# Two layer normalisations moved from VectorE to ScalarE, with scale and bias per token, in a post-norm attention and channel-mixing block

## The chip, the cores and the metric

One core of one Trainium2 chip runs the whole kernel. The metric is the time of one execution on the device in microseconds; the kernel before was timed three times, and the median of these counts.

## The reference

A batch of 16 sequences of 512 tokens with 128 channels goes through two sublayers. Each adds its input to its output and then normalises every token over its channels, without learned scale or shift:

```python
def _layernorm(x, axis=-1, eps=1e-05):
    m = jnp.mean(x, axis=axis, keepdims=True)
    v = jnp.var(x, axis=axis, keepdims=True)
    return (x - m) / jnp.sqrt(v + eps)
...
x = _layernorm(x + attn(x))      # 16 heads of 8 channels, causal softmax
x = _layernorm(x + ffn(x))       # token shift, r = sigmoid(xr Wr), relu(xk Wk)^2, r * (k Wv)
```

`attn` is multi-head attention with biases and an output projection. `ffn` mixes each token with the one before it per channel (`mu_r`, `mu_k`), and multiplies a sigmoid gate with a squared-ReLU path. Everything is float32.

## The kernel before, in words

The kernel is written by hand, one instruction stream per engine, with semaphores between them. It is a software pipeline over the 16 batch elements. Step b (from -3 to 17) handles six stages of different batch elements at once: X (load and transpose x) of element b+3, A (queries and keys) of b+2, S (scores for the row maxima) of b+1, T (transposed scores, exponentials, product with the values) of b, D (normalising the attention, projection, first layer normalisation) of b-1, and E (the feed-forward part and the second layer normalisation) of b-2. So full steps, with all of S, T, D and E, are those from 2 to 14; step 1 has D but no E, step 15 has no S, and steps 16 and 17 have D and E alone or E alone.

A step has 10 groups, 0 to 9, each with four chunks of 128 x 512 scores. The order inside a group is written out by hand in each engine's `step`:

- TensorE: two chunks of transposed scores (`tps`, L515), the mask matmuls (L538) and the scores for two row maxima (`sps`, L553), one small matmul job of the other stages; then the same for the other two chunks; at the end the product with the values (`ops`, L580) of the group before. Which small job comes where is the table `SPARE_USES`: `project` in group 5, the transposes `hT` in group 8.
- ScalarE: an exponential per chunk (`probs`, L677), two of them, then the copies due at this place, then two more. After group 9 two instructions `scaled` (L693) for the token shift.
- VectorE: a row maximum (`rowmax`, L747) per chunk of S, two, then other work, then two more. The first normalisation (y to `h`) stands after the first two row maxima of group 7, the second (z to `result`) after those of group 9. Each is four instructions on 128 x 128, one for each 128 tokens: `(src - mean) * rstd` with both as scalars per partition (L798).
- GpSimd: the causal mask of the exponentials (L850), the adds of residuals (`z`, `xbias`), the token-shift differences and sums, and `inverse_deviation`: `vareps = var + eps` (L870), then `rstd = vareps ** -0.5` (L872), for h in group 6, for z in group 7.
- SP issues the DMAs: loads of x, the bounce of queries, keys and maxima through device memory, and the store of `result`.

Both score buffers `tps` and `sps` have three banks. So two new chunks can be written when all but the last of the chunks before them have been read: chunks n and n+1 of `tps` wait until n-2 has gone through its exponential, and those of `sps` until n-2 has gone through its row maximum:

```python
wait(pe, exp_done, bank_free(n + 1))
...
wait(pe, s_reduced, bank_free(n + 1))
```

Each engine runs its own stream strictly in order, so an instruction put between two exponentials delays every later exponential by its own time, and a row maximum that is late delays the mask matmul of the next pair on TensorE with all that follows there.

Of the kernel before, what the change touches and what calls it, by code (L numbers as in the profile page):

```python
# [27 lines left out]
ACT = mybir.ActivationFunctionType  # L28
# [3 lines left out]
P = 128  # L32
# [53 lines left out]
def active(stage, b):  # L86

    return 0 <= b + OFFSET[stage] < BATCH


def before(stage, b):

    return min(max(b + OFFSET[stage], 0), BATCH)
# [77 lines left out]
def block_program(nc, x, W1, b1, Wp, bp, Wr, Wk, Wv, mu_r, mu_k, consts, out):  # L171
    with ExitStack() as ctx:
        def sb(name, shape, dt=F32):
            return ctx.enter_context(nc.sbuf_tensor(name, shape, dt))
# [4 lines left out]
        def sem(name):  # L179
            return ctx.enter_context(nc.semaphore(name))  # L180
# [41 lines left out]
        moments = sb("moments", [P, 2, TT, 2])  # L222
        vareps = sb("vareps", [P, 2, TT])
        rstd = sb("rstd", [P, 2, TT])
        h = sb("h", [P, 2, TT, E])
        hT = sb("hT", [P, SEQ + 1])
        step_d = sb("step_d", [P, SEQ])
# [53 lines left out]
        stats_done = sem("stats_done")  # L281
        moments_done = sem("moments_done")
        vareps_done = sem("vareps_done")
        rstd_done = sem("rstd_done")
        h_done = sem("h_done")
        step_done = sem("step_done")
# [11 lines left out]
        def wait(eng, semaphore, value):  # L298

            if value > 0:  # L300
                eng.wait_ge(semaphore, value)

        def is_written(eng, use, n, taken=None):

            if 0 <= n < BATCH and spare_bank(use, n) != taken:
                eng.wait_ge(spare_written[spare_bank(use, n)], COUNTS[use, n] + 1)
# [301 lines left out]
        def _(act):  # L608
# [76 lines left out]
            def split_middle(n, i):  # L685
                is_read(act, "qk"[i], n)
                nc.scalar.copy(part(i, 1), qk_rest[:, i, :]).then_inc(qk_middle, 1)  # L687

            def scale_steps(n):
                wait(act, step_done, n + 1)  # L690
                wait(act, mixed_done, 2 * n)
                for i in range(2):
                    nc.scalar.activation(scaled[:, i, :], step_d[:], ACT.Copy, scale=mus[:, i:i + 1])\  # L693
                        .then_inc(scaled_done, 1)

            def step(b):
                if b == 1 - OFFSET["A"]:
                    act.wait_ge(first_out[1], 16)
                    load_operand(act, b % 2 ^ 1, 0, 1, 1)
                    setup_rest()  # L700
                for g in range(GROUPS):
                    tb, tg = late(b, g)
                    for place in range(2):
                        if active("T", tb):
                            exp_chunk_of(before("T", tb), tg, 2 * place)
                            exp_chunk_of(before("T", tb), tg, 2 * place + 1)
                        for _, use, n in ORDER[b, g, place]:
                            spare_use(use, n)
                        if place == 0 and tg == 1 and active("D", tb):
                            copy_o(before("D", tb), 1)  # L710
                        if place == 0 and tg == CHUNKS + 1 and active("T", tb):
                            copy_o(before("T", tb), 0)
                    if g in (1, 2) and active("A", b) and before("A", b) > 0:
                        split_middle(before("A", b), g - 1)
                    if g in (0, 1) and active("A", b) and before("A", b) == 0:
                        split_middle(0, g)
                    if tg == 9 and active("D", tb):
                        scale_steps(before("D", tb))
# [5 lines left out]
        def _(dve):  # L724
# [35 lines left out]
            def spare_use(use, n):  # L760
                if use not in ("q", "k", "sums0", "sums1", "project", "value"):
                    return
                k = spare_bank(use, n)
                spare = spares[k]
                if use in ("q", "k"):
                    i = "qk".index(use)
                    wait(dve, qk_high, 2 * n + i + 1)
                    wait(dve, qk_split, 2 * (n - 1) + i + 1)
                    last = nc.vector.scalar_tensor_tensor(qk_rest[:, i, :], spare[:], bias[:, i:i + 1], part(i, 0),  # L769
                                                          ALU.add, ALU.subtract)  # L770
                elif use in ("sums0", "sums1"):

                    half = int(use[-1])
                    is_written(dve, use, n)
                    is_written(dve, "attnT", n - 1, k)
                    tiles = spare[:].rearrange("q (t r s h d) -> q s t r h d", t=TT, r=QUARTET, s=2, h=2)
                    nc.vector.reciprocal(inv[:, half], tiles[:, 1, :, :, :, 0]).then_inc(inv_done, 1)  # L777
                    wait(dve, inv_done, 2 * n + half + 1)
                    for t in range(TT):
                        last = nc.vector.tensor_tensor(  # L780
                            attn[:, t, DH * half:DH * half + DH].rearrange("q (r h) d -> q r h d", h=2),
                            tiles[:, 0, t], inv[:, half, t].unsqueeze(3).to_broadcast([P, QUARTET, 2, DH]), ALU.mult)
                elif use == "project":
                    wait(dve, xbias_done, n + 1)
                    is_written(dve, use, n)
                    last = nc.vector.tensor_tensor(y[:].rearrange("p t e -> p (t e)"), spare[:],
                                                   xbias[:].rearrange("p t e -> p (t e)"), ALU.add)
                elif use == "value":
                    wait(dve, z_done, n)
                    is_read(dve, "gate", n, k)  # L790
                    is_written(dve, use, n)
                    last = nc.vector.scalar_tensor_tensor(gated[:], gate[:], 1.0, spare[:], ALU.add, ALU.mult)  # L792
                last.then_inc(spare_read[k], 1)

            def normalise(i, n, src, dst, done_rstd, done):
                wait(dve, done_rstd, n + 1)
                for t in range(TT):
                    last = nc.vector.tensor_scalar(dst[:, t, :], src[:, t, :], moments[:, i, t, 0:1],  # L798
                                                   rstd[:, i, t:t + 1], ALU.subtract, ALU.mult)
                last.then_inc(done, 1)  # L800

            def step(b):
                for g in range(GROUPS):
                    tb, tg = late(b, g)
                    if active("S", b):
                        reduce_chunk(before("S", b), g, 0)
                        reduce_chunk(before("S", b), g, 1)
                    for _, use, n in ORDER[b, g, 0]:
                        spare_use(use, n)
                    if tg == 7 and active("D", tb):  # L810
                        n = before("D", tb)
                        wait(dve, z_done, n - 1)
                        normalise(0, n, y, h[:, n % 2], rstd_done, h_done)
                    if tg == 9 and active("E", tb):
                        n = before("E", tb)
                        wait(dve, stored, 16 * n)
                        normalise(1, n, z, result, rstd2_done, result_done)
                    if tg == 5 and active("D", tb):
                        n = before("D", tb)
                        is_read(dve, "project", n)  # L820
                        layer_norm_moments(y, 0, n, stats_done, moments_done)
                    if tg == 6 and active("E", tb):
                        n = before("E", tb)
                        wait(dve, z_done, n + 1)
                        layer_norm_moments(z, 1, n, stats2_done, moments2_done)
                    if active("S", b):
                        reduce_chunk(before("S", b), g, 2)
                        reduce_chunk(before("S", b), g, 3)
                    for _, use, n in ORDER[b, g, 1]:
                        spare_use(use, n)  # L830
# [5 lines left out]
        def _(pool):  # L836
# [22 lines left out]
            def split_max(n, half):  # L859
# [5 lines left out]
                nc.gpsimd.tensor_tensor(negmax_parts[:, 1, :], negmax[:], negmax_parts[:, 0, :], ALU.subtract)\  # L865
                    .then_inc(max_split, 1)

            def inverse_deviation(i, n, done_moments, done_eps, done_rstd):
                wait(pool, done_moments, n + 1)
                nc.gpsimd.tensor_scalar(vareps[:, i, :], moments[:, i, :, 1], EPS, None, ALU.add).then_inc(done_eps, 1)  # L870
                wait(pool, done_eps, n + 1)
                nc.gpsimd.tensor_tensor(rstd[:, i, :], vareps[:, i, :], half_power[:], ALU.pow).then_inc(done_rstd, 1)  # L872

            def mix_step(n):

# [77 lines left out]
```

## Time and profile before

| | |
|---|---|
| median of 3 runs | 742.22 us (741.91 to 744.46) |
| the profiled execution | 745.85 us, of which the span from first to last instruction is 744.1 us |
| TensorE / VectorE / ScalarE / GpSimd busy | 614.7 / 548.4 / 471.2 / 372.3 us |
| granted TensorE clock, mean | 0.963 of 2.4 GHz |
| one full step (period) | 40.17 us, from 264.64 to 304.81 |

Busy time counts instructions of an engine that overlap once. A row of the timeline gives the start in us, the length of the merged piece, the engine and line, the operation, output and inputs with shapes, a count, and in brackets how long the engine had been idle just before and what released it. A row of the chain gives start, length and what ran. PE is TensorE, DVE is VectorE, ACT is ScalarE, POOL is GpSimd.

### The profile page before, as it was taken

The page shows a single profiled execution, that of the slowest core. Times are in us where ns is not written, and L with a number is a line of the kernel's source. Part 1 is how long each engine was busy: PE and PEld are TensorE (multiplying, and loading weights), DVE is VectorE, ACT ScalarE, POOL GpSimd, SP SyncE. Part 2 cuts the span into 40 slices and gives each one's busy share as a digit, 9 for nine tenths or more (in the row PEclk, how much of TensorE's full clock was granted, in tenths as well). Part 3 has the DMA queues.
Part 4 walks back from the last instruction along what each step waited for, and adds up shares of the span by engine and source line. Part 5 has one row for each costly group of instructions (what it writes and reads, how often), then busy time and mean ns, then how long its engine had stood idle before and what let it go on. Part 6 is the DMA issues. An engine that isn't in the chain of part 4 may idle for free.

```text
span 744.1 us, 18019 instructions
## 1 busy us (share of the span) xinstructions
PE 614.7 (83%) x6727; PEld 277.9 (37%) x6727; DVE 548.4 (74%) x1642; ACT 471.2 (63%) x916; POOL 372.3 (50%) x519
## 2 busy tenths in 40 slices
PE   4468887898989899898989898989989898977643
PEld 2132333343443434353434344343434343433232
DVE  1477784879798888889797979888887979782231
ACT  2104773777768686767677776867686767677510
POOL 3011342455656565555655565646555565455623
PEclk9999997999999999999999999999999999999855
DMA  3421313131414223232313141413223231100100
GB/s 115 92 88 45 102 46 114 29 114 36 119 44 118 57 69 107 60 115 59 117 42 118 39 115 43 126 50 80 95 61 115 58 104 40 37 18 17 30 14 15
DMA packets 66014, 53.25 MB, mean 72 GB/s; under 512 B 11333, under 2 KB 61830, under 8 KB 65926
## 3 DMA queue, kind: packets, MB, share of 16 engines
q1 hardware_dynamic: 65198, 51.83, 25.2%
q8 instruction: 53, 0.87, 0.5%
q10 hardware_dynamic: 728, 0.26, 0.2%
q14 instruction: 35, 0.29, 0.1%
HBM read 34.70 MB, written 17.30 MB: 70 GB/s over the span
## 4 chain that ended last, share of the span: by engine, by line
PE 55%; DVE 18%; ACT 8%; issue 6%; POOL 6%; DMA 5%; SPq 1%; ACTq 1%; POOLq 0%; DVEq 0%
PE ops L580 14%; DVE rowmax L747 12%; PE sps L553 10%; PE tps L515 9%; PE spare L441 8%; ACT probs L677 5%; PE spare L459 4%; PE sps L538 3%; DVE h L798 3%; DMA xres<-L_attn_x 2%; POOL probs L850 2%; PE spare L491 2%; POOL mixed L883 2%; PE spare L475 2%; DMA d_max<-negmax_parts 1%
## 5 line engine op out<-in xcount | busy, mean ns | idle before, releaser
L747 DVE TENSOR_REDUCE rowmax<-sps 128x1 f32<-128x512 f32 (+7 forms) x1024 | 401.9, 450 | 101.6 <-PE sps L553 101.1
L677 ACT ACTIVATE probs<-tps 128x512 f32<-128x512 f32 x640 | 346.5, 596 | 147.1 <-PE tps L515 147.1
L850 POOL TENSOR_SCALAR_AFFINE_SELECT probs<-probs 128x512 f32<-128x512 f32 x256 | 158.8, 638 | 256.6 <-ACT probs L677 256.5
L580 PE MATMUL ops<-probs,vop 128*32 128x384 f32 (+3 forms) x2048 | 173.5, 446 | 8.1 <-POOL probs L850 6.8
L515 PE MATMUL tps<-qop,kop 50*128 50x384 bf16 (+3 forms) x1024 | 126.5, 305 | 40.3 <-ACT probs L677 36.5
L553 PE MATMUL sps<-kop,qop 48*64 48x512 bf16 (+7 forms) x2048 | 130.4, 310 | 8.4 <-DMA kop<-d_parts 8.4
L538 PE MATMUL sps<-qmask,dup 64*128 64x128 bf16 (+1 forms) x640 | 69.7, 214 | 33.0 <-DVE rowmax L747 28.7
L515 PEld LDWEIGHTS tps<-qop,kop 50*128 50x128 bf16 x1024 | 34.2, 94 | 161.3 <-ACT probs L677 115.2
L580 PEld LDWEIGHTS ops<-probs,vop 128*32 128x32 f32 x2048 | 50.7, 110 | 82.4 <-issue 61.4
L553 PEld LDWEIGHTS sps<-kop,qop 48*64 48x64 bf16 x2048 | 43.1, 106 | 50.5 <-issue 19.3
L538 PEld LDWEIGHTS sps<-qmask,dup 64*128 64x128 bf16 x640 | 31.4, 95 | 75.2 <-DVE rowmax L747 68.7
L857 POOL TENSOR_TENSOR qk_parts<-qk_rest,qk_parts 128x512 bf16<-128x512 f32 x32 | 36.9, 1153 | 29.4 <-ACT qk_parts L687 29.4
L459 PE MATMUL spare<-xT,w1p 128*128 128x512 f32 x62 | 39.6, 725 | 2.7 <-ACT xT L639 2.7
L883 POOL TENSOR_TENSOR mixed<-scaled,hT 128x512 f32<-128x512 f32 x32 | 39.9, 1272 | 0.8 <-ACT scaled L693 0.8
L769 DVE SCALAR_TENSOR_TENSOR qk_rest<-spare,bias,qk_parts 128x512 f32<-128x512 f32 x31 | 23.3, 752 | 21.4 <-ACT qk_parts L655 21.4
L655 ACT ACTIVATE qk_parts<-spare,bias 128x512 bf16<-128x512 f32 x31 | 21.3, 687 | 26.2 <-PE spare L459 26.2
L907 POOL TENSOR_TENSOR xbias<-xres,bias 128x512 f32<-128x512 f32 x16 | 20.3, 1268 | 33.9 <-DMA xres<-L_attn_x 33.9
L872 POOL TENSOR_TENSOR rstd<-vareps,half_power 128x4 f32<-128x4 f32 x32 | 33.4, 1043 | 2.7
L792 DVE SCALAR_TENSOR_TENSOR gated<-gate,spare 128x512 f32<-128x512 f32 x16 | 11.0, 688 | 31.2 <-PE spare L441 31.2
L777 DVE RECIPROCAL inv<-spare 128x32 f32<-128x32 f32 x32 | 11.2, 349 | 21.3 <-PE spare L475 21.3
L914 POOL TENSOR_TENSOR z<-gated,h 128x512 f32<-128x512 f32 x16 | 20.3, 1267 | 12.1 <-DVE gated L792 12.1
L491 PE MATMUL spare<-mixed,wffT 128*128 128x512 f32 x32 | 19.9, 705 | 6.0 <-POOL mixed L883 6.0
(72 smaller groups left out, 585.2 us busy)
## 6 DMA issues: line engine op xcount, KB each, us to landing
d_parts<-qk_parts SPq DMA_DIRECT2D x15, 768.0 KB, 3.7
qop<-d_parts SPq DMA_DIRECT2D x192, 32.0 KB
qop<-d_parts SPq DMA_DIRECT2D x64, 96.0 KB
kop<-d_parts SPq DMA_DIRECT2D x189, 32.0 KB
kop<-d_parts SPq DMA_DIRECT2D x63, 96.0 KB
xa<-L_attn_x SPq DMA_DIRECT2D x16, 256.0 KB, 3.0
xres<-L_attn_x SPq DMA_DIRECT2D x16, 256.0 KB, 3.4
out<-result SPq DMA_DIRECT2D x16, 256.0 KB, 2.5
```

Of the source, the lines that this page charges most:

```text
L441: last = nc.tensor.matmul(spare[:, P * t:P * t + P], tokensT[:, P * t:P * t + P], weights, start=True, stop=True)
L459: last = nc.tensor.matmul(spare[:], w1p[:, "qk".index(use), :], xT[:, par], start=True, stop=True)
L491: last = nc.tensor.matmul(spare[:], wffT[:, 1, :], mixed[:, 1, :], start=True, stop=True)
L515: last = nc.tensor.matmul(tps[:, bank(n + k), off:off + w], kop[r, par, pair, BLK * a:BLK * a + BLK], qop[r, par, pair, BLK * a:SEQ], star ...
L538: nc.tensor.matmul(dst, dup[r, :], src, start=True, stop=False, skip_group_check=True)
L553: last = nc.tensor.matmul(sps[out:out + QBLK, bank(n + k), off:off + w], qop[r, par, pair, QBLK * a:QBLK * a + QBLK], kop[r, par, pair, 0: ...
L580: last = nc.tensor.matmul(ops[32 * t:32 * t + 32, BLK * a:SEQ], vop[:, par, a, QUARTET * half + t, hh, :], probs[:, g % 2, i, off:off + w] ...
L677: nc.scalar.activation(probs[:, g % 2, i, :], tps[:, bank(n), :], ACT.Exp, scale=SCALE)\
L747: last = nc.vector.reduce_max(rowmax[:, par, QUARTET * half + i, a:a + 1], sps[:, bank(n), off:off + w], axis=AX_X)
L850: last = nc.gpsimd.affine_select(out=v, in_=v, compare_op=ALU.is_ge, fill=0.0, base=0, pattern=[[0, QUARTET], [1, BLK]], channel_multiplie ...
L857: nc.gpsimd.tensor_tensor(part(i, 2), qk_rest[:, i, :], part(i, 1), ALU.subtract).then_inc(qk_split, 1)
L883: nc.gpsimd.tensor_tensor(mixed[:, i, :], scaled[:, i, :], hT[:, 0:SEQ], ALU.add)\
```

## The change

The four instructions of each normalisation move from VectorE's stream to ScalarE's, in the same groups (7 and 9) and behind the first two exponentials there. They become an Identity activation `rstd * src + shift`, where `rstd` and `shift` are operands of one number per partition. GpSimd makes `shift = -(mean * rstd)` behind each `rstd`, by two more operations on 128 x 4 elements, each waiting for the one before on a new semaphore `powered`; `rstd_done` is now raised by the last of them. VectorE's add that writes y (`project`) gains a wait for the previous `h_done`, since y is now read by another engine. The waits for a free `h` or `result` buffer move to ScalarE with the instructions.

```diff
+            def normalise(i, n, src, dst, done_rstd, done):
+                wait(act, done_rstd, n + 1)
+                for t in range(TT):
+                    last = nc.scalar.activation(dst[:, t, :], src[:, t, :], ACT.Identity, bias=shift[:, i, t:t + 1],
+                                                scale=rstd[:, i, t:t + 1])
+                last.then_inc(done, 1)
...
                         for _, use, n in ORDER[b, g, place]:
                             spare_use(use, n)
+                        if place == 0 and tg == 7 and active("D", tb):
+                            n = before("D", tb)
+                            wait(act, z_done, n - 1)
+                            normalise(0, n, y, h[:, n % 2], rstd_done, h_done)
+                        if place == 0 and tg == 9 and active("E", tb):
+                            n = before("E", tb)
+                            wait(act, stored, 16 * n)
+                            normalise(1, n, z, result, rstd2_done, result_done)
...
                     is_written(dve, use, n)
+                    wait(dve, h_done, n)
                     last = nc.vector.tensor_tensor(y[:].rearrange("p t e -> p (t e)"), spare[:],
...
-            def normalise(i, n, src, dst, done_rstd, done):
-                wait(dve, done_rstd, n + 1)
-                for t in range(TT):
-                    last = nc.vector.tensor_scalar(dst[:, t, :], src[:, t, :], moments[:, i, t, 0:1],
-                                                   rstd[:, i, t:t + 1], ALU.subtract, ALU.mult)
-                last.then_inc(done, 1)
...
-                    if tg == 7 and active("D", tb):
-                        n = before("D", tb)
-                        wait(dve, z_done, n - 1)
-                        normalise(0, n, y, h[:, n % 2], rstd_done, h_done)
-                    if tg == 9 and active("E", tb):
-                        n = before("E", tb)
-                        wait(dve, stored, 16 * n)
-                        normalise(1, n, z, result, rstd2_done, result_done)
...
-                nc.gpsimd.tensor_tensor(rstd[:, i, :], vareps[:, i, :], half_power[:], ALU.pow).then_inc(done_rstd, 1)
+                nc.gpsimd.tensor_tensor(rstd[:, i, :], vareps[:, i, :], half_power[:], ALU.pow).then_inc(powered, 1)
+                wait(pool, powered, count)
+                nc.gpsimd.tensor_tensor(shift[:, i, :], moments[:, i, :, 0], rstd[:, i, :], ALU.mult).then_inc(powered, 1)
+                wait(pool, powered, count + 1)
+                nc.gpsimd.tensor_scalar(shift[:, i, :], shift[:, i, :], -1.0, None, ALU.mult).then_inc(done_rstd, 1)
```

ScalarE's order from group 6 to the start of the next step, in a full step, before (names are the kernel's tensors, output first, then the inputs; x6 is a count):

```order
L639 COPY xT<-spare 128x512
L677 ACTIVATE probs<-tps 128x512 x6
L662 COPY hT<-spare 128x512
L677 ACTIVATE probs<-tps 128x512 x6
L693 ACTIVATE scaled<-step_d,mus 128x512 x2
L677 ACTIVATE probs<-tps 128x512 x4
```

and the same place in the changed kernel:

```order
L641 COPY xT<-spare 128x512
L679 ACTIVATE probs<-tps 128x512 x2
L694 ACTIVATE h<-y,shift,rstd 128x128 x4
L679 ACTIVATE probs<-tps 128x512 x4
L664 COPY hT<-spare 128x512
L679 ACTIVATE probs<-tps 128x512 x4
L694 ACTIVATE result<-z,shift,rstd 128x128 x4
L679 ACTIVATE probs<-tps 128x512 x2
L702 ACTIVATE scaled<-step_d,mus 128x512 x2
L679 ACTIVATE probs<-tps 128x512 x4
```

The h group now stands behind two of the four exponentials of group 7, the result group behind two of the four of group 9, ahead of `scaled` and the next step's exponentials.

VectorE's order over the same groups, before:

```order
L753 BN_STATS stats<-z 128x6 x4
L757 BN_AGGR moments<-stats 128x2 x4
L747 TENSOR_REDUCE rowmax<-sps 128x1 x8
L798 TENSOR_SCALAR h<-y,moments,rstd 128x128 x4
L747 TENSOR_REDUCE rowmax<-sps 128x1 x12
L777 RECIPROCAL inv<-spare 128x32
L780 TENSOR_TENSOR attn<-spare,inv 128x64 x4
L747 TENSOR_REDUCE rowmax<-sps 128x1 x2
L798 TENSOR_SCALAR result<-z,moments,rstd 128x128 x4
L747 TENSOR_REDUCE rowmax<-sps 128x1 x6
```

and in the changed kernel:

```order
L770 BN_STATS stats<-z 128x6 x4
L774 BN_AGGR moments<-stats 128x2 x4
L764 TENSOR_REDUCE rowmax<-sps 128x1 x20
L794 RECIPROCAL inv<-spare 128x32
L797 TENSOR_TENSOR attn<-spare,inv 128x64 x4
L764 TENSOR_REDUCE rowmax<-sps 128x1 x8
```

Both groups have left VectorE, and the row maxima around them are neighbours now.

GpSimd's order in groups 6 and 7, before:

```order
L870 TENSOR_SCALAR vareps<-moments 128x4
L872 TENSOR_TENSOR rstd<-vareps,half_power 128x4
L850 AFFINE_SELECT probs<-probs 128x4x128 x2
L863 TENSOR_SCALAR negmax_parts<-negmax 32x128
L865 TENSOR_TENSOR negmax_parts<-negmax,negmax_parts 32x128
```

and in the changed kernel:

```order
L877 TENSOR_SCALAR vareps<-moments 128x4
L879 TENSOR_TENSOR rstd<-vareps,half_power 128x4
L881 TENSOR_TENSOR shift<-moments,rstd 128x4
L883 TENSOR_SCALAR shift<-shift 128x4
L853 AFFINE_SELECT probs<-probs 128x4x128 x2
```

The two operations for shift stand between rstd and the next mask of probs; the same holds for z's rstd in group 7.

## Rows read from the trace of the kernel before

**Rows 1.** The page: busy times, and the chain's shares by engine.

```profile
PE 614.7 (83%) x6727; PEld 277.9 (37%) x6727; DVE 548.4 (74%) x1642; ACT 471.2 (63%) x916; POOL 372.3 (50%) x519
...
PE 55%; DVE 18%; ACT 8%; issue 6%; POOL 6%; DMA 5%; SPq 1%; ACTq 1%; POOLq 0%; DVEq 0%
```

**Rows 2.** The chain of waits in order of time: start, us, what (VectorE, group 7).

```profile
135.83 1.45 DVE h L798 x4
...
256.43 1.35 DVE h L798 x4
257.78 0.67 DVE rowmax L747 x2
...
657.86 1.35 DVE h L798 x4
```

**Rows 3.** Timeline of TensorE, groups 8 and 0 of one period.

```profile
257.33 0.39 PE L515 MATMUL tps<-qop,kop 50*128 50x384 bf16 x4
258.50 0.23 PE L538 MATMUL sps<-qmask,dup 64*128 64x128 bf16 x2 [0.78 <-DVE rowmax L747]
...
259.59 0.39 PE L515 MATMUL tps<-qop,kop 50*128 50x384 bf16 x4
259.92 0.23 PE L538 MATMUL sps<-qmask,dup 64*128 64x128 bf16 x2
...
266.41 0.39 PE L515 MATMUL tps<-qop,kop 50*128 50x512 bf16 x2 [0.92 <-ACT probs L677]
```

**Rows 4.** Timeline of ScalarE, groups 7 and 9 of the same period.

```profile
254.48 2.16 ACT L677 ACTIVATE probs<-tps 128x512 f32<-128x512 f32 x4 [0.60 <-PE tps L515]
...
262.49 2.16 ACT L677 ACTIVATE probs<-tps 128x512 f32<-128x512 f32 x4 [1.22 <-PE tps L515]
264.54 1.33 ACT L693 ACTIVATE scaled<-step_d,mus 128x512 f32<-128x512 f32 x2
```

**Rows 5.** Groups of instructions on ScalarE: count, busy us and mean ns, idle before.

```profile
L626 ACT ACTIVATE wffT<-tps 128x128 f32<-128x128 f32 x1 | 0.3, 285 | 0.0
L693 ACT ACTIVATE scaled<-step_d,mus 128x512 f32<-128x512 f32 x32 | 21.3, 721 | 1.1 <-POOL step_d L877 1.1
L687 ACT CAST qk_parts<-qk_rest 128x512 bf16<-128x512 f32 x32 | 19.8, 618 | 2.0 <-DVE qk_rest L769 2.0
L655 ACT ACTIVATE qk_parts<-spare,bias 128x512 bf16<-128x512 f32 x31 | 21.3, 687 | 26.2 <-PE spare L459 26.2
L677 ACT ACTIVATE probs<-tps 128x512 f32<-128x512 f32 x640 | 346.5, 596 | 147.1 <-PE tps L515 147.1
```

**Rows 6.** Timeline of GpSimd, group 6 of the next period.

```profile
289.69 0.23 POOL L870 TENSOR_SCALAR vareps<-moments 128x4 f32<-128x4 f32 x1
290.00 1.05 POOL L872 TENSOR_TENSOR rstd<-vareps,half_power 128x4 f32<-128x4 f32 x1
293.65 1.23 POOL L850 TENSOR_SCALAR_AFFINE_SELECT probs<-probs 128x512 f32<-128x512 f32 x2 [2.60 <-ACT probs L677]
```

**Rows 7.** Step 15 on ScalarE and TensorE, and the last h in the chain.

```profile
689.75 2.16 ACT L677 ACTIVATE probs<-tps 128x512 f32<-128x512 f32 x4 [0.54 <-PE tps L515]
...
691.73 0.39 PE L515 MATMUL tps<-qop,kop 50*128 50x384 bf16 x4
...
720.14 1.13 DVE h L798 x4
```

**Rows 8.** Stretches: length, busy time of PE, PEld, DVE, ACT, POOL, granted clock, DMA.

```profile
264.73:266.41 1.68, 0.76 (x13) 0.31 (x10) 1.37 (x4) 1.68 (x4) 1.68 (x3) 1.00 0.51 146
...
697.95:699.45 1.50, 0.03 (x4) 0.03 (x5) 0.00 (x0) 1.33 (x3) 1.31 (x3) 1.00 0.49 151
699.45:701.25 1.80, 1.75 (x16) 0.56 (x16) 0.00 (x0) 0.00 (x0) 1.80 (x2) 0.55 0.55 162
...
119.97:129.86 9.89, 9.89 (x65) 5.29 (x66) 4.41 (x13) 2.82 (x6) 3.03 (x5) 0.51 0.26 79
284.59:290.42 5.83, 5.63 (x65) 3.23 (x64) 4.65 (x14) 2.82 (x6) 3.64 (x6) 1.00 0.53 120
```

More of the change, by code:

```diff
@@ L224, in block_program @@
         rstd = sb("rstd", [P, 2, TT])
+        shift = sb("shift", [P, 2, TT])
         h = sb("h", [P, 2, TT, E])
@@ L283, in block_program @@
         vareps_done = sem("vareps_done")
+        powered = sem("powered")
         rstd_done = sem("rstd_done")
@@ L866, in split_max @@
                     .then_inc(max_split, 1)
+            powers = [0, 0]
             def inverse_deviation(i, n, done_moments, done_eps, done_rstd):
+                count = 2 * (powers[i] + powers[1 - i]) + 1
+                powers[i] = n + 1
                 wait(pool, done_moments, n + 1)
```

## The prediction

> **What bounds the kernel now.** I read the page first [rows 1]: TensorE is busy for 83% of the span, VectorE for 74%, ScalarE for 63%, and the chain that ended last is TensorE for 55% and VectorE for 18%. No engine is saturated; the time is a ring of short waits around TensorE, repeated in a period of 40.2 us. So the question is not how much work leaves VectorE, but which waits end on it. The chain of waits in order of time [rows 2] shows one: the four instructions that normalise h lie on the chain once in each of the 14 periods from 135.8 to 657.9 us, with the row maxima queued behind them. The timeline of TensorE [rows 3] shows the cost. After the score matmuls of 257.33 the mask matmul starts at 258.50, idle for 0.78 us for VectorE; with no wait that step takes 259.92 - 259.59 = 0.33 us, so the whole stall is 258.50 - 257.33 - 0.33 = 0.84 us. The normalising of result (group 9) is never on the chain.
>
> In group 9 the ring closes over ScalarE instead. Its timeline [rows 4] shows four exponentials packed without a gap (2.16 us from 262.49), then the two scaled instructions (1.33 us), and the second pair of score matmuls of group 0 waits 0.92 us, until 266.41, for the exponential that follows them [rows 3]. What is inserted between those four exponentials reaches TensorE undiminished.
>
> **The change part by part.** All times are those of the period from 254 to 295 us.
>
> *Price of one normalising ACTIVATE.* No row has 128 columns and both pointers; I build it from rows [rows 5]. 128 columns without pointers take 285 ns. A scale per partition adds 721 - 618 = 103 ns, a bias per partition 687 - 596 = 91 ns. Both: 479 ns. Neighbours overlap: the four exponentials give (2.16 - 0.596)/3 = 0.52 us from start to start, 0.08 less than one lasts; the two scaled ones 1.33 - 0.72 = 0.61, which is 0.11 less. With 0.10 an ACTIVATE costs 0.38 us, four delay the next instruction by 1.52 us, and the last of four ends 3 x 0.38 + 0.48 = 1.62 us after the first starts. Bounds: 0.29 us (four 1.16) if the pointers are fetched together, 0.42 us (four 1.68) if reading SBUF adds 20 ns and only 0.08 overlaps. I take 0.38, because both increments are measured, each alone.
>
> The Trainium skill, page "ScalarE: Activation LUTs", section "What ACT_TABLE_LOAD costs", says that each pointer operand adds about 93 ns and that neighbours overlap by about 93 ns. By it one would cost 0.39 us, four 1.54, and the sum below would be +18.9 us in place of +18.3; no row here shows two pointers in one instruction.
>
> *Group 7, h leaves VectorE.* The row maxima after S(7) follow at once and are done by 257.1, so the mask matmul no longer waits for VectorE. But ScalarE now has h between its second and third exponential: the third started at 254.48 + 2 x 0.52 = 255.52 [rows 4]; now at 257.04, and ends 0.60 later, at 257.64. The score matmuls of group 8 need it (three banks), so they start at 257.69 and not 257.33, and the mask matmul 0.33 later at 258.02. Gain: 258.50 - 258.02 = 0.48 us of the 0.84; the new wait eats the rest. h itself ends at 255.52 + 1.62 = 257.14, before its transposes. 14 periods: **-6.7 us**.
>
> *Group 9, result goes between the exponentials.* The third exponential, the fourth, both scaled instructions and the first exponential of group 0 all stand behind it in ScalarE's queue. All move by 1.52 us and TensorE's second pair of score matmuls with them. result runs in 13 periods with both matmul streams: **+19.8 us**. What VectorE is spared there is worth nothing: no one waited for it. Net per period: +1.04 us.
>
> *Step 15* has scores but no row maxima: VectorE was not in the way, so nothing is won. The third exponential of group 7 now ends at 689.75 + 1.04 + 1.52 + 0.60 = 692.91, and the matmuls of 691.73 [rows 7] start at 692.96: +1.23; group 9 again +1.52. **+2.75 us**.
>
> *GpSimd.* Two operations on 128 x 4 elements follow each rstd. The nearest row is vareps: 0.23 us, 0.31 from its start to that of rstd [rows 6]. So +0.62 each time. For h, rstd ends at 291.05, shift at 291.67, and GpSimd then waits anyway until 293.65. For z it delays one mask of probs by 0.6 us, whose matmuls come a whole group later. Nothing in steps 1 to 15; without that cover it would be 0.62 us on the path. That happens in the tail.
>
> *Tail.* For the last batch rstd, shift, normalise stand in line twice. Each time +0.62 for shift and 1.62 - 1.12 = 0.50 for the slower four [rows 7]; result of the batch before now also delays scaled by 0.3. **+2.5 us**.
>
> *Queues and waits moved.* The store of result is SP's next item after result_done, with the operand loads behind it; result ends at most 0.2 us later than before, while the groups that use those loads move by 1.04. The project step's new wait on h_done is for the previous batch, long over; VectorE's wait for rstd is gone. Nothing for either.
>
> Sum: -6.7 + 19.8 + 2.75 + 2.5 = **+18.3 us**. The profiled execution took 745.85 us, 3.6 above the median of 742.22; the sum is added to the median: 760.5. With 0.29 us per ACTIVATE the gain is the full 0.84 (-11.8), the loss 15.1, step 15 2.0, the tail 1.5: +6.9, 749.1. With 0.42: -4.5 + 21.8 + 3.1 + 2.9 = +23.3, 765.5.
>
> *TensorE's clock.* The delay lands as a hole in TensorE's work. From the end of its PV matmuls in group 8 (264.25 in the new order) to the late score matmuls (267.45) it has 0.76 us of work, that of the row 264.73:266.41 [rows 8], and 2.4 us of idling. Near the end of the trace the clock fell from 2.4 to 1.2 GHz after a shorter hole: TensorE is busy for 0.03 us of the 1.5 after 697.95, and then the granted clock goes to 0.55 [rows 8]. The price of a fall: 65 matmuls from 119.97 took 9.89 us at clock 0.51; the same 65 take 5.83 at full clock [rows 8]: 4.06 us. So none of the 13 new holes costs a clock, or up to all do: 0 to 53 us. I take five, +20.3, between the two: the one place alike fell, and the 0.92 us wait that stands in every period before never did. **Total: 742.2 + 18.3 + 20.3 = 780.8 us.**
>
> **The rivals.**
> *The holes cost no clock.* Then 760.5 us, between 749.1 and 765.5. For it: the fall is one place in a tail where TensorE has little work anyway. Against it: the new hole is deeper than that one, and comes every period.
> The page "TensorE: Matmul & The Clock Gate" of the Trainium skill, section "Why this matters for your kernels", warns only of long idle gaps between bursts of matmuls. By that rule no new hole would cost a clock and the time is this rival's; the fall near 699.6, after 1.5 us, speaks against the rule.
>
> *Not slower: pointer fetches are hidden.* If consecutive ACTIVATEs prefetch their scale and bias, one costs 0.285 - 0.10 = 0.185 us and four 0.74. The third exponential of group 7 then never delays TensorE, and the full 0.84 us is won against 0.74 lost: -0.84 (the one period without result) - 13 x 0.10 + 1.2 (step 15) + 0.7 (tail) = -0.3 us, 742 us. The point that decides is four in 0.84 us, 0.21 each. Against it: the two scaled instructions stand 0.61 apart and exponentials of the same width 0.52, so a pointer shows even in a pair.
>
> *The change doesn't free VectorE where it counts.* If the mask matmul then waited for something else as long, the 6.7 us would be missing: 767 us without a clock. ScalarE's row makes that half true already.
>
> **How the numbers follow.** Slower with clock falls 0.55, slower without 0.33, even 0.12. The likeliest is 780.8, its own range 765 to 815 (one to thirteen falls, and a little for step 15). The whole range, 749 to 815, takes in the second case down to its cheapest ACTIVATE and leaves out the even case. A measurement tells about 0.5% (3.7 us) from no change. Slower 0.88; same 0.09; faster 0.03, from the even case with a still cheaper ACTIVATE.
>
> **What would show it.** In the lines of the new profile: h and result on ScalarE with a mean near 0.48 us, 0.38 apart. TensorE's mask matmul at the start of group 8 no longer waits for VectorE, its score matmuls wait briefly for ScalarE. The second pair of group 0 waits about 1.5 us for ScalarE, not 0.92. A period of 41.2 us where the clock stays at 1.0, about 45 where it falls; in stretches of 10 us, values near 0.5 right after group 9. ScalarE busy 471 + 128 x 0.48 = 532 us. The prediction is wrong if the period stays at 40.2, if the ACTIVATEs stand 0.2 us apart, or if a clock of 1.0 holds while the period is still far over 41.2.

## The result, and the profile after

The changed kernel is slower: a ratio of 1.0263 to the kernel before, 95% interval 1.0214 to 1.0312. The median of its six runs is 769.4 us (757.7 to 774.6), that of the kernel before, timed beside it, 745.1. The ratio leaves out runs more than 1.5% above the fastest of their kernel, here the three longest of the change. The forecast was 780.8 us, range 749 to 815, slower with 0.88.

The page of the profiled execution (763.36 us, span 761.6) answers to [rows 1]:

```profile
PE 622.0 (82%) x6727; PEld 278.0 (36%) x6727; DVE 511.2 (67%) x1514; ACT 515.8 (68%) x1044; POOL 386.1 (51%) x583
...
PE 58%; ACT 17%; DVE 11%; issue 5%; POOL 3%; DMA 3%; SPq 1%; ACTq 1%; DVEq 0%; POOLq 0%
L694 ACT ACTIVATE h<-y,shift,rstd 128x128 f32<-128x128 f32 x64 | 26.2, 487 | 9.3 <-POOL shift L883 9.3
L694 ACT ACTIVATE result<-z,shift,rstd 128x128 f32<-128x128 f32 x64 | 26.3, 488 | 7.7 <-POOL shift L883 7.7
```

VectorE has 37 us less to do and ScalarE 45 us more, and they have changed places in the chain: VectorE from 18% to 11%, ScalarE from 8% to 17%. One ACTIVATE with both pointers (`rstd` and `shift`, the operands of one number per partition) lasts 487 ns; 479 was built from [rows 5].

Where the period gained and lost shows in TensorE's timeline, groups 8 to 0, which answers to [rows 3]. The first line is the key matmul of the step's group 2, the last that of the next step; I use it as the mark of a period.

```profile
278.22 1.13 PE L493 MATMUL spare<-mixed,wffT 128*128 128x512 f32 x2
...
301.93 0.39 PE L517 MATMUL tps<-qop,kop 50*128 50x384 bf16 x4 [0.23 <-ACT probs L679]
302.15 0.22 PE L540 MATMUL sps<-qmask,dup 64*128 64x128 bf16 x2
...
305.65 0.39 PE L517 MATMUL tps<-qop,kop 50*128 50x256 bf16 x4
...
309.38 0.39 PE L517 MATMUL tps<-qop,kop 50*128 50x512 bf16 x2 [0.93 <-ACT probs L679]
...
311.48 0.39 PE L517 MATMUL tps<-qop,kop 50*128 50x512 bf16 x2 [1.34 <-ACT probs L679]
...
319.15 1.12 PE L493 MATMUL spare<-mixed,wffT 128*128 128x512 f32 x2
```

The same marks in the kernel before:

```profile
233.92 1.12 PE L491 MATMUL spare<-mixed,wffT 128*128 128x512 f32 x2
...
262.00 0.39 PE L515 MATMUL tps<-qop,kop 50*128 50x256 bf16 x4
...
274.08 1.12 PE L491 MATMUL spare<-mixed,wffT 128*128 128x512 f32 x2
```

The mask matmul of group 8 no longer waits for VectorE; the score matmuls ahead of it now wait 0.23 us for ScalarE. From the mark to the start of group 9 it was 262.00 - 233.92 = 28.08 us and is 305.65 - 278.22 = 27.43: 0.65 won. From there to the second score pair of group 0 it was 266.41 - 262.00 = 4.41 [rows 3] and is 311.48 - 305.65 = 5.83: 1.42 lost. The first pair of group 0, which did not wait before, now waits 0.93 us. These two waits, with 0.76 us of matmuls between them, are the hole behind group 9. The period grows from 40.16 to 40.93 us.

ScalarE's timeline has the cause in its order [rows 4 for before]:

```profile
298.78 1.08 ACT L679 ACTIVATE probs<-tps 128x512 f32<-128x512 f32 x2 [0.59 <-PE tps L517]
299.75 1.64 ACT L694 ACTIVATE h<-y,shift,rstd 128x128 f32<-128x128 f32 x4
301.29 2.21 ACT L679 ACTIVATE probs<-tps 128x512 f32<-128x512 f32 x4
...
306.14 1.08 ACT L679 ACTIVATE probs<-tps 128x512 f32<-128x512 f32 x2 [1.17 <-PE tps L517]
307.11 1.64 ACT L694 ACTIVATE result<-z,shift,rstd 128x128 f32<-128x128 f32 x4
308.65 1.07 ACT L679 ACTIVATE probs<-tps 128x512 f32<-128x512 f32 x2
309.61 1.33 ACT L702 ACTIVATE scaled<-step_d,mus 128x512 f32<-128x512 f32 x2
310.83 2.16 ACT L679 ACTIVATE probs<-tps 128x512 f32<-128x512 f32 x4
```

Four ACTIVATEs of 1.64 us delay the next exponential by 1.54 (299.75 to 301.29, 307.11 to 308.65), so one costs 0.385 us. Behind result stand two exponentials, scaled, and the next step's exponentials without a gap.

The third part is the clock. Of the eleven periods between steps 2 and 13, nine last 40.92 to 41.21 us and two longer, 43.70 and 42.46. These stretches of 1 us cover the hole in the second of the two (columns as in [rows 8]):

```profile
225.00:226.00 1.00, 0.07 (x6) 0.04 (x3) 0.00 (x0) 1.00 (x3) 0.00 (x0) 1.00 0.00 0
226.00:227.00 1.00, 0.75 (x8) 0.21 (x8) 0.21 (x1) 1.00 (x3) 0.60 (x2) 1.00 0.61 181
227.00:228.00 1.00, 0.00 (x0) 0.00 (x0) 1.00 (x2) 1.00 (x3) 1.00 (x3) 1.00 0.61 177
228.00:229.00 1.00, 0.91 (x8) 0.25 (x8) 0.08 (x1) 0.92 (x3) 1.00 (x2) 0.63 0.63 146
229.00:230.00 1.00, 1.00 (x5) 0.50 (x2) 0.76 (x2) 0.69 (x2) 1.00 (x1) 0.50 0.67 110
```

TensorE works 0.82 us of three, and then its clock falls from 2.4 to 1.2 GHz, for the matmuls of group 0 that are the chain. The waits are the same, to 0.01 us, as in the period shown above, in which the clock held:

```profile
225.99 0.39 PE L517 MATMUL tps<-qop,kop 50*128 50x512 bf16 x2 [0.93 <-ACT probs L679]
...
228.09 0.49 PE L517 MATMUL tps<-qop,kop 50*128 50x512 bf16 x2 [1.34 <-ACT probs L679]
```

### The profile page after: what moved, and what is told of

Read it like the earlier page. It is cut to its first block, busy times and chain, and to the rows that moved or that the text cites. A ratio compares the mean times of both kernels' runs of the same rounds, so it can differ in the third digit from the quotient of the medians.

```text
span 761.6 us, 18083 instructions
## 1 busy us (share of the span) xinstructions
PE 622.0 (82%) x6727; PEld 278.0 (36%) x6727; DVE 511.2 (67%) x1514; ACT 515.8 (68%) x1044; POOL 386.1 (51%) x583
## 4 chain that ended last, share of the span: by engine, by line
PE 58%; ACT 17%; DVE 11%; issue 5%; POOL 3%; DMA 3%; SPq 1%; ACTq 1%; DVEq 0%; POOLq 0%
PE ops L582 15%; PE spare L443 10%; PE sps L555 9%; PE tps L517 9%; ACT probs L679 8%; DVE rowmax L764 7%; PE spare L461 5%; ACT h L694 3%; PE sps L540 3%; ACT result L694 3%; PE spare L493 2%; PE spare L477 1%; ACT scaled L702 1%; PE spare L490 1%; PE spare L482 1%
## 5 line engine op out<-in xcount | busy, mean ns | idle before, releaser
L582 PE MATMUL ops<-probs,vop 128*32 128x384 f32 (+3 forms) x2048 | 176.7, 453 | 6.5 <-POOL probs L853 5.4
L517 PE MATMUL tps<-qop,kop 50*128 50x384 bf16 (+3 forms) x1024 | 128.4, 309 | 60.8 <-ACT probs L679 57.1
L540 PE MATMUL sps<-qmask,dup 64*128 64x128 bf16 (+1 forms) x640 | 70.0, 215 | 22.2 <-DVE rowmax L764 18.3
L461 PE MATMUL spare<-xT,w1p 128*128 128x512 f32 x62 | 41.5, 757 | 2.7 <-ACT xT L641 2.7
L918 POOL TENSOR_TENSOR xbias<-xres,bias 128x512 f32<-128x512 f32 x16 | 20.3, 1270 | 26.9 <-DMA xres<-L_attn_x 26.9
L694 ACT ACTIVATE h<-y,shift,rstd 128x128 f32<-128x128 f32 x64 | 26.2, 487 | 9.3 <-POOL shift L883 9.3
L694 ACT ACTIVATE result<-z,shift,rstd 128x128 f32<-128x128 f32 x64 | 26.3, 488 | 7.7 <-POOL shift L883 7.7
```

What stands on the lines that cost most here:

```text
L461: last = nc.tensor.matmul(spare[:], w1p[:, "qk".index(use), :], xT[:, par], start=True, stop=True)
L517: last = nc.tensor.matmul(tps[:, bank(n + k), off:off + w], kop[r, par, pair, BLK * a:BLK * a + BLK], qop[r, par, pair, BLK * a:SEQ], star ...
L540: nc.tensor.matmul(dst, dup[r, :], src, start=True, stop=False, skip_group_check=True)
L582: last = nc.tensor.matmul(ops[32 * t:32 * t + 32, BLK * a:SEQ], vop[:, par, a, QUARTET * half + t, hh, :], probs[:, g % 2, i, off:off + w] ...
L694: last = nc.scalar.activation(dst[:, t, :], src[:, t, :], ACT.Identity, bias=shift[:, i, t:t + 1], scale=rstd[:, i, t:t + 1])
```

## The experiments

Two theories were set against each other. A: the place of the four ACTIVATEs in ScalarE's stream decides, and the hole behind group 9 costs the clock beside it. B: the added load on ScalarE and GpSimd costs the time, wherever it stands. "Period" is the usual interval of the mark; a fall of the clock shows as a longer one.

**e1 and e2: one normalisation each.** In e1 result goes back to VectorE, in e2 h does (and with it goes the new wait on `h_done`).

```diff
-                        if place == 0 and tg == 9 and active("E", tb):   # e1: on ScalarE no longer
+                    if tg == 9 and active("E", tb):                      # e1: on VectorE
...
-                        if place == 0 and tg == 7 and active("D", tb):   # e2: likewise h
+                    if tg == 7 and active("D", tb):
```

> h is normalised on ScalarE as in the change, result on VectorE as before. Theory A (what counts is where the four ACTIVATEs stand in ScalarE's stream): the gain of the changed kernel's group 8 stays (0.65 us in each of 14 periods) and group 9's loss is gone. Period 39.5 us, no hole behind group 9 and no fall of the clock there; step 15 and the tail give 2 to 3 us back. About 6.5 us faster than before, ratio 0.991. Theory B (the load on ScalarE and the longer chain on GpSimd cost the time wherever they stand): half of the loss stays, ratio about 1.013.

> result is normalised on ScalarE between the exponentials of group 9, h on VectorE as before. Theory A: period 40.17 + 1.42 = 41.6 us, the wait of the second score pair of group 0 for ScalarE at 1.3 us, and VectorE still ahead of the mask matmul in group 8 with 0.78 us. 13 periods 18.5, step 15 and tail 3: about 21 us slower without falls of the clock, ratio 1.03; with falls up to 1.05. Theory B: half of the change's loss, ratio about 1.013.

e1: ratio 0.9912 (0.9879 to 0.9945), period 39.52 us, no fall in steps 2 to 14. e2: ratio 1.0528 (1.0468 to 1.0588); where the clock holds the period is 41.26, not 41.6, and eight of eleven are 42.8 to 44.2. Gains and losses add up: e1's 39.52 and the 1.42 of group 9 make 40.94 (the change: 40.93). For e2, the expectation left out what GpSimd's part wins by itself: the 39.85 of e6 below and 1.42 make 41.27. So the change is a good half and a bad one: h alone wins, result alone costs more than both together. B falls. One of e2's falls, around its hole and to the end of the slow stretch:

```profile
351.00:353.00 2.00, 0.76 (x8) 0.26 (x8) 1.11 (x2) 2.00 (x4) 1.49 (x3) 0.98 0.59 174
353.00:359.40 6.40, 6.20 (x40) 1.84 (x40) 2.22 (x4) 2.87 (x6) 2.78 (x3) 0.50 0.65 112
```

With these 6.4 us at half clock this period took 44.04 us, 2.8 more than 41.26; the shorter falls cost 1.5 to 1.8.

**e5, e8, e10: the hole filled.** TensorE repeats a score matmul four times in each wait of group 0, into a bank that the real one then overwrites. e5 is the change with it, e8 is e2 with it, e10 the kernel before with it.

```diff
+                if g == 0 and 2 <= batch < BATCH - 1:
+                    wait(pe, exp_done, bank_free(n))
+                    for _ in range(FILL):          # 4
+                        nc.tensor.matmul(tps[:, bank(n), :], kop[HROWS * 0:TERMS + MROWS, par, 0, 0:BLK],
+                                         qop[HROWS * 0:TERMS + MROWS, par, 0, :], start=True, stop=True)
                 wait(pe, exp_done, bank_free(n + 1))
```

> The changed kernel, and TensorE repeats a score matmul four times in each of the two waits of group 0 (steps 2 to 14), into a bank that the real matmul then overwrites. If the holes cost the clock: no fall behind group 9 in steps 2 to 14, every period 40.9 us, the median near 759 us (ratio 1.019) and the runs within some 6 us, not 17. If the clock has no part in it: median 769 and a spread as before; if the extra matmuls themselves delay, a period over 40.9.

> e2 with the repeated score matmuls of e5 in the two waits of group 0. In e2 eight of the eleven intervals between steps 2 and 13 were over 41.3 us (42.8 to 44.2). If falls of the clock made those: every interval 41.3 us, the median some 17 us lower than e2's 783, near 766. If something else made them: the same long intervals, about 783.

> The kernel before with the repeated score matmuls of e5. There is no fall of the clock behind group 9 to prevent, and the wait of 0.92 us has room for the four of them: the same time as before, ratio 0.998 to 1.004, period 40.2. If the repeats help or hurt by themselves, it differs, and e5 and e8 have to be read with that.

e5: median 761.0 us, six runs from 757.9 to 764.1 (the change: 757.7 to 774.6), periods of 40.95 us, one of 41.24, and no fall in steps 2 to 14. But its ratio, 1.0258 (1.0207 to 1.0308), can't be told from the change's 1.0263, and the two profiled executions took the same time, 763.21 and 763.36 us. The medians of all runs against those of before are 1.0246 here and 1.0326 there, so e5 points the way that was expected and does not show it. e8 does: 766.7 us where e2 took 783.2, ratio 1.0288 (1.0243 to 1.0334) against 1.0528, with ten periods of 41.24 to 41.53 and one of 42.86 instead of eight long ones. Work that computes nothing made the kernel 16 us faster. The eleven periods of e2 and of e8 as one stretch each, with the granted clock at 0.96 and at 1.00:

```profile
151.15:622.85 471.70, 417.24 (x4629) 184.04 (x4621) 360.48 (x1078) 337.14 (x672) 262.29 (x397) 0.96 0.29 77
```

```profile
155.58:611.22 455.64, 421.15 (x4716) 187.46 (x4708) 360.00 (x1078) 336.91 (x672) 261.64 (x397) 1.00 0.29 79
```

In e5, the hole looks like this:

```profile
306.78 1.03 PE L514 MATMUL tps<-qop,kop 50*128 50x512 bf16 x4
307.69 0.39 PE L523 MATMUL tps<-qop,kop 50*128 50x512 bf16 x2
...
308.38 1.03 PE L514 MATMUL tps<-qop,kop 50*128 50x512 bf16 x4
309.88 0.39 PE L523 MATMUL tps<-qop,kop 50*128 50x512 bf16 x2 [0.47 <-ACT probs L685]
```

L514 are the repeats: they fit and the wait of 1.34 is down to 0.47. e10 missed its expectation: 753.4 us, ratio 1.013 (1.0097 to 1.0163), period 40.89. I had overlooked that the kernel before has only one of the two waits; ahead of the first score pair of group 0 TensorE is busy, so four repeats of 0.2 us each lie on the path there. That is what e5 and e8 don't suffer, since their periods are those of the unfilled kernels. So filling pays only where the hole is.

**e7: no pointers.** The change with ACTIVATEs of constant scale and without bias.

```diff
-                    last = nc.scalar.activation(dst[:, t, :], src[:, t, :], ACT.Identity, bias=shift[:, i, t:t + 1],
-                                                scale=rstd[:, i, t:t + 1])
+                    last = nc.scalar.activation(dst[:, t, :], src[:, t, :], ACT.Copy, scale=1.5)
```

> The changed kernel with ACTIVATEs that have a constant scale of 1.5 and no bias, so h and result are 1.5 times y and z. If the two pointers make the price: one lasts 0.29 to 0.31 us, four delay by 0.8 and not 1.52; score matmuls of group 8 not delayed (1.0 us won), 0.7 us lost in group 9: period 39.9 us, ratio about 0.996. If it is the four instructions and their waits as such: period 40.9, ratio 1.02.

One lasts 310 ns; the pointers cost 177 ns together, close to the 194 that [rows 5] give for two fetches, so they add up and aren't shared. (The function also changes, from Identity to Copy; its share was not measured alone.) The period is 39.91 us, as expected; but seven of eleven periods are 41.4 to 41.9, with falls of the clock, and the ratio is 1.0126 (1.0069 to 1.0183), not 0.996. Here the first wait of group 0 is short and the second as long as in the change:

```profile
301.56 0.39 PE L517 MATMUL tps<-qop,kop 50*128 50x512 bf16 x2 [0.20 <-ACT probs L679]
...
303.67 0.39 PE L517 MATMUL tps<-qop,kop 50*128 50x512 bf16 x2 [1.34 <-ACT probs L679]
```

**e6 and e11: GpSimd's part alone.** Both normalisations on VectorE as before, GpSimd makes shift and no one reads it. In e11 z's two operations stand behind the mask of group 7.

```diff
                         count = inverse_deviation(1, before("E", tb), moments2_done, vareps2_done, rstd2_done)
...
                         mask_group(before("T", tb), tg)
+                    if tg == 7 and active("E", tb):       # e11
+                        make_shift(1, count, rstd2_done)
```

> Both normalisations on VectorE as before; GpSimd makes shift as in the change, and rstd_done comes only after it. If GpSimd's two operations are hidden: period 40.2 us, 1.2 us more in the tail, ratio 1.002. If they are on the path: 0.6 us in each of 14 periods, ratio 1.012.

> As e6, with z's two shift operations behind the mask of probs of group 7 on GpSimd and no longer ahead of it. The period of e6 was 39.85 us against 40.17 before, and the fourth ACTIVATE-sized piece of h on VectorE lasted about 340 ns where it lasted over 660 before. If the mask running beside it made it slow: here the mask starts as early as before, that instruction is slow again and the period is 40.17. If something else in e6 won the 0.32 us: 39.85.

e6: ratio 0.9974 (0.9941 to 1.0006), but the period is 39.85 us, 0.32 shorter than before, where 40.2 was expected. The tail pays 1.2 us, as expected. The reason for the shorter period stands in VectorE's lines. In the kernel before, and in e6:

```profile
256.35 1.43 DVE L798 TENSOR_SCALAR h<-y,moments,rstd 128x128 f32<-128x128 f32 x4
...
257.00 0.70 POOL L850 TENSOR_SCALAR_AFFINE_SELECT probs<-probs 128x512 f32<-128x512 f32 x1
```

```profile
291.78 1.11 DVE L800 TENSOR_SCALAR h<-y,moments,rstd 128x128 f32<-128x128 f32 x4
...
292.97 0.64 POOL L852 TENSOR_SCALAR_AFFINE_SELECT probs<-probs 128x512 f32<-128x512 f32 x1
```

Before, GpSimd's mask starts beside the fourth instruction of h, and the four take 1.43 us; in e6 the two new operations push the mask behind them, and the four take 1.11. e11 puts the mask back and keeps all work: period 40.24, mean of h 434 ns (e6: 363), ratio 1.002 (0.9981 to 1.0058). So it is the mask running beside h that makes it slow. One instruction of the four bears all of it, the fourth before and the third in e11; the others take about 0.34 us. Before, it ends 0.08 us behind the mask (257.78 and 257.70). The first line is from before, the second from e11:

```profile
257.11 0.67 DVE L798 TENSOR_SCALAR h<-y,moments,rstd 128x128 f32<-128x128 f32 x1
```

```profile
292.89 0.76 DVE L800 TENSOR_SCALAR h<-y,moments,rstd 128x128 f32<-128x128 f32 x1
```

One period of the kernel before shows the same without any edit: the mask started 0.93 us after h instead of 0.65, the four took 1.10 us, and the period lasted 39.84 us (475.36 to 515.20).

```profile
497.79 1.10 DVE L798 TENSOR_SCALAR h<-y,moments,rstd 128x128 f32<-128x128 f32 x4
...
498.72 0.67 POOL L850 TENSOR_SCALAR_AFFINE_SELECT probs<-probs 128x512 f32<-128x512 f32 x1
```

In e11's expectation "ACTIVATE-sized" is a slip; the piece is VectorE's.

**e3, e4, e9: other places on ScalarE.** e3 is e1 with h behind the fourth exponential of group 7; e9 has three of h's four behind the second and one behind the third. e4 has both normalisations on ScalarE, h as in e3 and result behind the fourth exponential of group 8.

```diff
-                        if place == 0 and tg == 7 and active("D", tb):
+                        if place == 1 and tg == 7 and active("D", tb):   # e3, e4
...
-                        if place == 0 and tg == 9 and active("E", tb):
+                        if place == 1 and tg == 8 and active("E", tb):   # e4
...
+                        if place == 1 and tg == 7 and active("D", tb):   # e9, after the third exponential
+                            normalise(0, n, y, h[:, n % 2], rstd_done, h_done, 3, TT)
```

> As e1, but h stands behind all four exponentials of group 7 (where ScalarE sat idle for 1.17 us before) instead of behind two. Theory A: the score matmuls of group 8 no longer wait for ScalarE, the whole stall of 0.84 us and the mask's own 0.17 are won: period 39.2 us, about 12 us faster than before, ratio 0.984. Theory B: no different from e1.

> Both normalisations on ScalarE, h behind the fourth exponential of group 7, result behind the fourth of group 8 (where ScalarE sat idle for 1.22 us). Theory A: h wins 1.0 us, result delays the first exponential of group 9 by about 0.5: period 39.7 us, ratio 0.990 to 1.0. Theory B: the same work on the same engines as the change, so its ratio of 1.026.

> As e1, with three of h's four ACTIVATEs behind the second exponential of group 7 and the fourth behind the third. In e1 the third exponential held up the score matmuls of group 8, in e3 the last ACTIVATE held up the transposes of h by 0.2 us; here neither should wait. Period 39.2 us, some 3 us less than e1 and e3, about 733 us, ratio 0.986. If ScalarE's work as such is the limit and not the place: no better than e3 (39.4).

e3: ratio 0.9889 (0.9844 to 0.9935), period 39.42 and not 39.2. The score matmuls no longer wait, but the transposes of h do:

```profile
329.90 0.39 PE L517 MATMUL tps<-qop,kop 50*128 50x384 bf16 x4
...
330.87 0.63 PE L490 MATMUL spare<-cst,h 128*128 128x128 f32 x4 [0.18 <-ACT h L694]
```

e4: ratio 0.9919 (0.9878 to 0.996), period 39.69. It has the same instructions on the same engines as the change, and is faster than the kernel before where the change is 2.6% slower. This is the cleanest case against B. e9: ratio 0.9883 (0.9846 to 0.9919), period 39.30 and not 39.2; its period is the best of all, while its whole time can't be told from e1's and e3's. All four are about 1% faster than the kernel before.

| | period, clock held | ratio |
|---|---|---|
| before | 40.17 | 1 |
| change | 40.93 | 1.026 |
| e1 h on ScalarE / e2 result on ScalarE | 39.52 / 41.26 | 0.991 / 1.053 |
| e5 change, filled / e8 e2, filled | 40.95 / 41.25 | 1.026 / 1.029 |
| e7 change without pointers / e10 before, filled | 39.91 / 40.89 | 1.013 / 1.013 |
| e3, e9, e4: other places | 39.42, 39.30, 39.69 | 0.989, 0.988, 0.992 |
| e6, e11: shift alone | 39.85, 40.24 | 0.997, 1.002 |

## Why the prediction was right or wrong

*The price of an ACTIVATE* was right: 0.38 us forecast, 0.385 measured, 479 and 487 ns long. Both pointers are paid. The Trainium skill's page "ScalarE: Activation LUTs", section "What ACT_TABLE_LOAD costs" (some 93 ns for each pointer), agrees with the trace within some 5 ns a pointer: 487 with two, 310 with none. ScalarE's busy time was forecast at 532 us and is 515.8: the forecast added each ACTIVATE at its full length, and neighbours overlap (the two rows of L694 are busy for 52.5 us, not 61).

*Group 7* gave 0.65 us per period, not 0.48. The mechanism was as described: the score matmuls wait for the third exponential. Two sizes were off. The first line is from the kernel before, the second from the changed one; each is the last matmul group ahead of group 8:

```profile
256.33 1.07 PE L580 MATMUL ops<-probs,vop 128*32 128x384 f32 x16
```

```profile
300.63 1.07 PE L582 MATMUL ops<-probs,vop 128*32 128x384 f32 x16
```

From there the score matmuls started after 1.00 us (257.33) and start after 1.30 (301.93), so they are late by 0.30 and not by the 0.36 of the sum (257.69 less 257.33). And the mask matmul follows them after 0.22 us (302.15), where the sum took 0.33 from the second pair of group 8. The whole stall was therefore 1.17 less 0.22, 0.95 us and not 0.84, and 0.95 less 0.30 is the 0.65. e6 shows that about half of this, 0.32, would have come without moving h at all, because shift moves GpSimd's mask away from VectorE's h (39.85 there, 39.52 in e1).

*Group 9* lost 1.42 us per period, 1.52 forecast, by the path named: third and fourth exponential, scaled, first exponential of the next step, second score pair. ScalarE's own line has the 1.42: from the first exponential of group 9 to scaled it takes 3.47 us (306.14 to 309.61) where it took 2.05 (262.49 to 264.54). The wait shows at both score pairs of group 0, 0.93 and 1.34 us, where the prediction named about 1.5 at the second. result now lies on the chain of waits in each of the 13 periods:

```profile
307.50 1.25 ACT result L694 x3
```

Net it was 0.76 per period, not 1.04.

*GpSimd* in steps 1 to 15 was put at nothing. The two operations take 0.20 and 0.24 us and hide, as said; that they help by 0.32 was not foreseen.

*The tail* was right: step 16 took 1.40 us more (27.11 against 25.71 from mark to mark), 1.42 forecast, the end 1.09, 1.12 forecast. Step 15 with 3.46 was above the 2.75, with the clock at 0.5 for part of it.

*The sum without the clock*, +18.3 us, is what e5 comes to, whose holes are filled in steps 2 to 14: 761.0 - 742.7 = +18.3 by the medians, 17.4 by the profiled executions. That it fits so well is partly luck: the two terms of the period were each off by 0.1 to 0.2. Mark to mark, the 13 periods from step 2 to step 15 took 10.5 us more in e5 than before, where the sum has 13.5 (13 times 1.04); step 15 took 4.1 more, where the sum has 2.75. In both the clock was at 0.5 for a part (674.2 to 683.3 and 701.5 to 708.1).

*The clock* is where the number went wrong, in size. The mechanism was right: the holes do make the clock fall, e2 against e8 shows it. In the profiled executions it fell in 10 of the 22 periods of e2 and the change, and in one of the 22 of e8 and e5. But a fall was priced at 4.06 us, from the one long slow stretch of the trace [rows 8]; in the groups behind the hole one costs 1.5 to 2.8 us (42.46 and 43.70 against 40.93). And there were two of them in steps 2 to 13 of the profiled execution, not five: 4.3 us instead of 20.3. Over all runs the medians of the change and of e5, each against its own before, differ by 0.8%, some 6 us, but the ratios don't tell the two apart. How often the clock fell in the other runs of the change isn't known, since one execution of it was profiled. The same kernel without a fall was the rival "the holes cost no clock", 760.5; the result lies between the two. The section of the Trainium skill's page "TensorE: Matmul & The Clock Gate" that the prediction names, "Why this matters for your kernels", warns of long idle gaps between bursts of matmuls, and that is not the whole rule here: the trace shows a fall after waits of 0.93 and 1.34 us with 0.76 us of work between.

*The rivals*: "pointer fetches are hidden" is refuted by 0.385 us apart. "The change doesn't free VectorE where it counts" is refuted for the mask matmul and true in part for the pair ahead of it.

What stays open is why the clock falls in eight of eleven periods of e2, seven of e7 and two of the change, when the waits of the change and e2 are the same to 0.01 us, in periods with and without a fall, and the first wait of e7 is only 0.20; the traces show where it fell, not what decides it.

## What to carry to other kernels

Before work is moved to a less busy engine, look at which instruction it will stand in front of: here the same eight instructions on the same engine cost 2.6% behind the second exponential and win 0.8% behind the fourth, where that engine was idle anyway. Take off the critical engine what is on the chain and leave what isn't: h paid, result was never waited for. And count a hole in TensorE's work not only as its own length: a clock that falls in it is paid in the dense groups behind (1.5 to 2.9 us a time here).

## What had not been expected of the hardware

A GpSimd mask that runs beside VectorE's four tensor-scalar instructions makes them take 1.43 us and not 1.11, and two small GpSimd operations ahead of the mask make the period 0.32 us shorter; with the mask back beside them it is 40.24 us again. And matmuls whose results are thrown away made e2 16 us faster (783.2 to 766.7) by keeping the clock at 2.4 GHz in all but one of eleven periods, while in the kernel before, where TensorE had no hole at one of the two places, the same matmuls cost 10 us.
